# Causal maxima over blocks of 128 keys, a residual summed by a transfer, and the gate's logits copied before the next maximum

## The reference

```python
x = layernorm(x + local_attention(x))     # 16 heads of 8, each query sees itself and the 128 keys before it
x = layernorm(x + block(x))
# block: h = ln1(x); causal attention of h, 16 heads of 8, all earlier keys
#        x_resid = x + o @ w_o
#        moe_in = ln2(x_resid); probs = softmax(moe_in @ w_gate) over 8 experts; the best 2, renormalised
#        out = sum over the 2 of gate * (gelu(moe_in @ w1[e] + b1[e]) @ w2[e] + b2[e])
#        return out + x_resid
```

## Time and profile before

| | |
|---|---|
| median of 3 runs | 785.24 us (781.52 to 786.43) |
| the profiled execution | 784.6 us, its span 782.8 us, mean granted clock of TensorE 0.938 |
| PE busy | 632.5 us (81%) |
| DVE busy | 565.3 us (72%) |
| ACT busy | 461.5 us (59%) |
| POOL busy | 423.6 us (54%) |
| iterations 0 to 7 (local) | about 46 to 281 us |
| iterations 8 to 15 (causal) | about 281 to 586 us |
| experts and last norm | about 586 to 783 us |

### The profile page before, as it was taken

How to read it: one execution, slowest core, us unless ns; L and a number is a source line. 1 busy time by engine, 2 the same in 40 slices (tenths; PEclk the granted TensorE clock), 3 DMA queues, 4 the chain that set the end, 5 groups by cost and what they waited for, 6 DMA issues and landing times.

```text
span 782.8 us, 20450 instructions
## 1 busy us (share of the span) xinstructions
PE 632.5 (81%) x7679; PEld 386.4 (49%) x7679; DVE 565.3 (72%) x1302; ACT 461.5 (59%) x757; POOL 423.6 (54%) x646
## 2 busy tenths in 40 slices
PE   3568989988998788888888889888777996999760
PEld 1333444544454343444444434444337996899760
DVE  2655677877877989897879887989633784655573
ACT  2035666766765566766676767666773572555443
POOL 5026567666755544244646474657765556544672
PEclk8568999999999999999999999999998998999995
DMA  6745734754551626343526261710111223222745
GB/s 191 185 112 101 178 120 87 190 139 100 135 153 26 176 95 124 103 93 97 126 69 154 66 157 41 183 44 18 55 48 46 59 60 96 63 70 62 146 72 161
DMA packets 57549, 82.22 MB, mean 105 GB/s; under 512 B 7672, under 2 KB 48096, under 8 KB 54380
## 3 DMA queue, kind: packets, MB, share of 16 engines
q1 hardware_dynamic: 51228, 68.78, 35.0%
q0 software_dynamic: 5184, 11.61, 6.0%
q10 hardware_dynamic: 1040, 0.52, 0.2%
HBM read 43.55 MB, written 37.17 MB: 103 GB/s over the span
## 4 chain that ended last, share of the span: by engine, by line
PE 44%; DVE 17%; issue 11%; DMA 10%; ACT 8%; POOL 5%; SPq 3%; another core or an unknown queue 1%; POOLq 0%; DVEq 0%; ACTq 0%
PE side_ps L1473 9%; PE pair_ps L1622 8%; PE pair_ps L1634 7%; DMA arena<-parts_dram 5%; PE pair_ps L1393 4%; ACT probs L753 4%; PE pair_ps L1494 4%; DVE row_max L928 3%; POOL rows_dram L657 2%; DVE row_max L930 2%; DMA rows_dram<-rows,row_at 2%; DVE rest L951 2%; DMA arena<-shift_t 2%; PE pair_ps L1418 2%; PE pair_ps L1453 2%
## 5 line engine op out<-in xcount | busy, mean ns | idle before, releaser
L753 ACT ACTIVATE probs<-pair_ps 128x1024 f32<-128x1024 f32 x272 | 275.9, 1021 | 126.4 <-PE pair_ps L1393 123.2
L1473 PE MATMUL side_ps<-probs,v_aug 128*32 128x256 f32 (+3 forms) x2048 | 162.2, 412 | 9.1 <-POOL probs L645 4.0
L879 ACT ACTIVATE arena<-pair_ps,arena 128x128 f32<-128x128 f32 x284 | 81.0, 369 | 83.9 <-PE pair_ps L1622 60.4
L1393 PE MATMUL pair_ps<-arena 50*128 50x256 bf16 (+3 forms) x1024 | 107.6, 286 | 27.5 <-DMA arena<-shift_t 7.5
L632 POOL TENSOR_SCALAR_AFFINE_SELECT probs<-probs 128x512 f32<-128x512 f32 x96 | 61.4, 640 | 119.1 <-ACT probs L753 118.2
L698 POOL DMA_INDIRECT outputs_dram<-arena x71 | 71.0, 1000 | 73.4 <-DVE arena L1274 50.6
L919 DVE TENSOR_REDUCE row_max<-pair_ps 128x4 f32<-128x768 f32 x96 | 88.9, 950 | 26.4 <-PE pair_ps L1427 25.8
L1622 PE MATMUL pair_ps<-arena 128*128 128x128 f32 x568 | 80.3, 287 | 19.1 <-issue 10.1
L1393 PEld LDWEIGHTS pair_ps<-arena 50*128 50x128 bf16 x1024 | 32.4, 95 | 107.6 <-issue 43.7
L1622 PEld LDWEIGHTS pair_ps<-arena 128*128 128x128 f32 x568 | 73.0, 201 | 21.8 <-issue 21.7
L928 DVE TENSOR_REDUCE row_max<-pair_ps 128x2 f32<-128x1024 f32 x64 | 76.5, 1219 | 9.3 <-PE pair_ps L1453 7.7
(11 more groups left out here) (178 smaller groups left out, 1033.1 us busy)
## 6 DMA issues: line engine op xcount, KB each, us to landing
arena<-parts_dram SPq DMA_DIRECT2D x96, 192.0 KB
parts_dram<-parts SPq DMA_DIRECT2D x32, 384.0 KB
parts_dram<-parts SPq DMA_DIRECT2D x32, 256.0 KB
pack<-in_pack SPq DMA_DIRECT2D x8, 578.0 KB, 10.4
arena<-rows_dram SPq DMA_DIRECT2D x71, 65.0 KB
parts_dram<-parts SPq DMA_DIRECT2D x32, 128.0 KB
arena<-parts_dram SPq DMA_DIRECT2D x32, 128.0 KB
resid<-outputs_dram POOLq DMA_DIRECT2D x6, 512.0 KB
```

The source lines that it names most:

```text
L753: nc.scalar.activation(probs[:, n % PROBS, :], pair_ps[RING_AT["score", n][0]][:, :, :].rearrange("p b t -> p (b t)"), ACT.Exp, scale=SCAL ...
L879: last = nc.scalar.activation(hidden[n % H_DEPTH][:, f * BLK:(f + 1) * BLK], hidden_ps[n % 2][:, f * BLK:(f + 1) * BLK], ACT.Gelu_apprx_ta ...
L1393: last = nc.tensor.matmul(pair[:, r, col:col + width], k_st[u % STACKS][own, gs, j * P:(j + 1) * P], q_st[u % STACKS][own, gs, q0:q0 + wid ...
L1473: last = nc.tensor.matmul(o_ps[c * VHEAD:(c + 1) * VHEAD, q0:q0 + width], v_aug[u % 2][:, j, first:first + VHEAD], probs[:, slot, r * T + ...
```

## The change

Three edits, all in the causal units.

1. *Mixed pairs.* Each mixed pair is laid out as four blocks of 128 keys: queries 0 to 127 now stand in block 0 and the three blocks of queries 256 to 383 in blocks 1 to 3. One reduction writes a maximum per block, four per head slot, into a wider `row_max` (13 rows of results in place of 4). As queries 256 to 383 then have three partial maxima, `split_shift` first merges the three by one more reduction in SBUF, and waits for it. TensorE's mask product covers blocks 0 and 3 in place of 2 and 3, and the short product comes before the long one; their number and sizes stay.
2. *The residual.* GpSimd's addition of y into `resid` becomes an accumulating transfer on GpSimd's queue. `sum_ready` counts in sixteens.
3. *The logits.* The copy out of `misc` becomes a function of its own, `take_logits`. In step 16 VectorE runs it ahead of that step's maximum; the search for the two best stays behind it.

```diff
--- before.py
+++ after.py
@@ -272,7 +272,7 @@
         parts = sb("parts", [P, PARTS, 2, T], BF16)
         rest = sb("rest", [P, 2, T])
         v_aug = [sb(f"v_aug{i}", [P, NT, VROW]) for i in range(2)]
-        row_max = [sb(f"row_max{i}", [P, NT, TILES_R, GS]) for i in range(2)]
+        row_max = [sb(f"row_max{i}", [P, 3 * NT + 1, TILES_R, GS]) for i in range(2)]
         shift = sb("shift", [P, NT, TILES_R, 2, GS], BF16)
         shift_t = sb("shift_t", [4 * GS, T], BF16)
         probs = sb("probs", [P, PROBS, 2 * T])
@@ -382,7 +382,7 @@
         middle_ready, low_ready = sem("middle_ready"), sem("low_ready")
         stored_high, stored_low = sem("stored_high"), sem("stored_low")
         stack_in = [sem(f"stack_in{i}") for i in range(STACKS)]
-        max_filled, max_done = sem("max_filled"), sem("max_done")
+        max_filled, max_done, max_merged = sem("max_filled"), sem("max_done"), sem("max_merged")
         shift_hi, shift_lo = sem("shift_hi"), sem("shift_lo")
         shift_in = [sem(f"shift_in{i}") for i in range(STACKS)]
         score_filled, exp_done, masked = sem("score_filled"), sem("exp_done"), sem("masked")
@@ -670,7 +670,7 @@
 
                 b = w - B
                 pool.wait_ge(misc_taken, JOB["out", w])
-                nc.gpsimd.tensor_tensor(resid[:, b, :, :], y[:, :, :], resid[:, b, :, :], ALU.add).then_inc(sum_ready, 1)
+                nc.gpsimd.dma_start(resid[:, b, :, :], y[:, :, :], accum_op=ALU.add).then_inc(sum_ready, 16)
 
             for it in ITERATIONS:
                 w = it - 1
@@ -706,7 +706,7 @@
             def add_outputs(share, choice):
 
                 if (share, choice) == (0, 0):
-                    pool.wait_ge(sum_ready, B)
+                    pool.wait_ge(sum_ready, B * 16)
                     for i in range(X_DEPTH):
                         pool.wait_ge(y_out[i], len(range(i, SETTLED, X_DEPTH)) * 16)
                 if choice:
@@ -927,20 +927,25 @@
                 if m < 2:
                     nc.vector.tensor_reduce(top[:, 3, :, 2 * g + m], pair[:, :, :], AX_X, ALU.max).then_inc(max_done, 1)
                 elif m < 4:
-                    nc.vector.tensor_reduce(top[:, 2, :, 2 * g + m - 2], pair[:, :, 0:3 * P], AX_X, ALU.max)
-                    nc.vector.tensor_reduce(top[:, 0, :, 2 * g + m - 2], pair[:, :, 3 * P:T], AX_X, ALU.max).then_inc(max_done, 1)
+                    nc.vector.tensor_reduce(top[:, 0:3 * NT + 1:NT, :, 2 * g + m - 2], pair[:, :, :].rearrange("p b (n k) -> p n b k", k=P),
+                                            AX_X, ALU.max).then_inc(max_done, 1)
                 else:
                     nc.vector.tensor_reduce(top[:, 1, :, 2 * g:2 * g + 2], pair[:, :, :].rearrange("p b (s k) -> p b s k", k=2 * P),
                                             AX_X, ALU.max).then_inc(max_done, 1)
 
             def split_shift(u):
 
+                tops = row_max[u % 2][:, 0:NT, :, :]
                 dve.wait_ge(max_done, BEFORE[u + 1])
+                if layer(u) == CAUSAL:
+                    thirds = row_max[u % 2][:, NT:3 * NT + 1:NT, :, :]
+                    nc.vector.tensor_reduce(tops[:, 2, :, :], thirds.rearrange("p n r g -> p r g n"), AX_X, ALU.max).then_inc(max_merged, 1)
+                    dve.wait_ge(max_merged, u - B + 1)
                 if u:
                     dve.wait_ge(misc_filled, JOB["shift", u - 1])
-                nc.vector.tensor_scalar(shift[:, :, :, 0, :], row_max[u % 2][:, :, :, :], -1.0, None, ALU.mult).then_inc(shift_hi, 1)
+                nc.vector.tensor_scalar(shift[:, :, :, 0, :], tops, -1.0, None, ALU.mult).then_inc(shift_hi, 1)
                 dve.wait_ge(shift_hi, u + 1)
-                nc.vector.scalar_tensor_tensor(out=shift[:, :, :, 1, :], in0=row_max[u % 2][:, :, :, :], scalar=-1.0,
+                nc.vector.scalar_tensor_tensor(out=shift[:, :, :, 1, :], in0=tops, scalar=-1.0,
                                                in1=shift[:, :, :, 0, :], op0=ALU.mult, op1=ALU.subtract).then_inc(shift_lo, 1)
 
             def split_rest(u):
@@ -984,7 +989,7 @@
                     dve.wait_ge(x1_ready, B)
                     if b:
                         dve.wait_ge(applied, b)
-                        dve.wait_ge(sum_ready, b)
+                        dve.wait_ge(sum_ready, b * 16)
                     nc.vector.tensor_tensor(y[:, :, :], proj, resid[:, b, :, :], ALU.add).then_inc(misc_taken, 1)
 
             def moments(w):
@@ -1028,14 +1033,15 @@
                                                        ALU.subtract, ALU.mult)
                     last.then_inc(applied, 1)
 
-            def top_two(w):
-
-                b = w - B
-                done = b * len(ROUTE)
-                if b:
-                    dve.wait_ge(routed, done)
+            def take_logits(w):
+
+                if w > B:
+                    dve.wait_ge(routed, (w - B) * len(ROUTE))
                 dve.wait_ge(misc_filled, JOB["logits", w])
                 nc.vector.tensor_copy(logits[:, :, :].rearrange("p t e -> p (t e)"), misc[:, 0:NT * E]).then_inc(misc_taken, 1)
+
+            def top_two(w):
+
                 dve.wait_ge(misc_taken, JOB["logits", w])
                 for t in range(NT):
                     last = nc.vector.max(top_val[:, t, :], logits[:, t, :])
@@ -1229,6 +1235,8 @@
                         divide(w)
                     if "out" in before:
                         add_input(before["out"])
+                    if "logits" in before:
+                        take_logits(before["logits"])
                     for u, m in MAXIMA.get((it, k), ()):
                         maximum(u, m)
                     if project_at(it, k - 1) is not None:
@@ -1324,6 +1332,7 @@
                 if m == CHAIN["apply"]:
                     apply(LAST)
                 if m == CHAIN["logits"]:
+                    take_logits(LAST)
                     top_two(LAST)
                 if m == CHAIN["choose"]:
                     choose(LAST)
@@ -1431,18 +1440,15 @@
                     return
                 g, m = m // 5, m % 5
                 if m < 2:
-                    work, masked_cols = [(2 * g + m, 3, T, 0)], slice(3 * P, T)
+                    work, masked_blocks = [(2 * g + m, 3, T, 0)], slice(3, 4)
                 elif m < 4:
-                    work, masked_cols = [(2 * g + m - 2, 2, 3 * P, 0), (2 * g + m - 2, 0, P, 3 * P)], slice(2 * P, T)
+                    work, masked_blocks = [(2 * g + m - 2, 0, P, 0), (2 * g + m - 2, 2, 3 * P, P)], slice(0, 4, 3)
                 else:
-                    work, masked_cols = [(2 * g + s, 1, 2 * P, s * 2 * P) for s in range(2)], None
+                    work, masked_blocks = [(2 * g + s, 1, 2 * P, s * 2 * P) for s in range(2)], slice(1, 4, 2)
                 for half in range(2):
                     for r in range(TILES_R):
                         own = slice(HALF * r, HALF * (r + 1))
-                        if masked_cols is None:
-                            target = pair[:, r, :].rearrange("p (s k) -> p s k", k=2 * P)[:, :, P:2 * P]
-                        else:
-                            target = pair[:, r, masked_cols].rearrange("p (s k) -> p s k", k=P)
+                        target = pair[:, r, :].rearrange("p (s k) -> p s k", k=P)[:, masked_blocks, :]
                         keys = slice(HALF * half, P)
                         nc.tensor.matmul(target[:, :, keys], eye_b[own, HALF * (1 - half):HALF * (1 - half) + P],
                                          first_b[r][own, half, keys].unsqueeze(1).to_broadcast([HALF, target.shape[1], P - HALF * half]),
```

## The result

On the chip where the prediction was settled the changed kernel's median is 779.86 us against 785.13 us for the kernel before (18 runs each; 17 of the runs after lie from 776.96 to 781.80, and one execution of 1907.68 us stands outside and is not in the ratio): the ratio is 0.9932, 95% interval 0.9915 to 0.9948. Two more comparisons of the same two kernels gave 0.9941 (0.9914 to 0.9968) and 0.9929 (0.9902 to 0.9957). The forecast was 779.4 us. The gain is real, and under 1%. The profiled execution's span is 775.7 us, 7.1 us less than that of before.

The account below looks back on a forecast made before the run. The prediction took TensorE and VectorE, both nearly full in causal iterations and handing each other the maxima, as the bound. 784.6 - 3.4 - 1.5 - 0.9 = 778.8 us profiled, so a 779.4 us median; 8-in-10 range 772.5 to 786.5.

Parts of the forecast that it names:

- The logits: Step 16 of causal iterations: the copy moved past one maximum removes TensorE's 0.85 us stall in five iterations; 3.4 us gained.
- The clock: Behind step 16: with the stall gone, falls to 1.2 GHz become fewer; 1.5 us gained, bounds 2.5 gained and 2.5 lost.
- new falls would turn up elsewhere: Sign of being wrong: new falls of the clock in the local units or the experts, which the change doesn't touch.
- The mixed pairs: VectorE's mixed-pair reductions: 1.13 us from start to start, 0.06 less each, against small merges; 0.9 us gained.
- The residual: GpSimd's 1.28 us addition becomes a transfer's issue; 0 gained, bounds 1 us gained and 1 lost.
- the blocks cost more than two instructions: Rival, chance 0.1: each bank change costs VectorE, the reduction may take 1.6 us; total 792 us.
- the stall is only exchanged: Rival, chance 0.15: ScalarE, next to be late, holds TensorE and the clock falls as before; total 783.5 us.
- the clock doesn't hang on this stall: Rival, chance 0.1: the falls come from how the whole iteration is filled; total 780.9 us.
- More of it counts: Rival, chance 0.2: all clock falls go, the stall counts in full, plus VectorE's 2.3 us and 1 from the shift; 775.2 us.

Follow-up runs that it names:

- after_again: The changed kernel with all three edits, measured once more against the kernel before on the chip of other follow-up kernels: ratio 0.9941.
- after_third: The changed kernel with all three edits, measured again against the kernel before on a third chip: ratio 0.9929.
- logits_only: The kernel before with only the copy of the logits moved ahead of step 16's maximum: 758.03 us against 764.67, ratio 0.9923.
- mixed_only: The kernel before with only the mixed pairs in one reduction, plus the merge and TensorE's mask order: 762.75 us, ratio 0.9972.
- no_residual: The changed kernel with the residual's addition back on GpSimd: 779.37 us against the changed kernel's 782.3; ratio 0.9908 to the kernel before.
- rows_later_2: Repeat of the changed kernel with ScalarE's copy of the rows one step later: 777.26 us against the changed kernel's 782.3; 0.9865 of the kernel before.

## Why the prediction was right

The forecast was 779.4 us and 779.86 was measured. The mechanism was the forecast one, the stall for the logits and the clock behind it; that the number came out within 0.5 us is luck, since the terms measured one by one come to 8 us where 5.8 were forecast and 5.3 measured. By its own steps:

- **The logits** were put at 3.4 us, and the clock at 1.5. Alone the edit measured 5.9 (3.6 to 8.3), where the two steps are 4.9. The step was right in kind and low in size: the stall was worth 1.04 us and not 0.85, and 0.21 went back in each iteration and not 0.28 in three, which gives 5 x 0.83 = 4.1 us. How it goes back was read wrong. The prediction had ScalarE take 0.28 us in three iterations, and two in which the one-hot choice moves up by all of the stall and makes it good. At the exponential 0.34 us are taken back (2.32 us behind the turn, against 1.98), but the choice decides in all five: its end moves up by 0.81 of the 1.04 us, as GpSimd's masks, which follow ScalarE, stretch it from 0.44 to 0.69 us. In the two iterations of before in which TensorE shows a wait for it, that wait is 0.31 us now in place of 0.45, and the ranking still comes 0.21 us later behind the turn.
- **The clock.** The falls behind step 16 are gone in every trace. Three stood in the trace of before, 2.5 us by the prediction's count; the four kernels with the stall have 1.75 on average, at 1.0 us for a whole one, which is nearer to the 1.5 taken. By the rule cited from the Trainium skill (TensorE: Matmul & The Clock Gate, Part 1), taken alone, a half-busy array would have kept its clock; the runs show otherwise, with 7 falls behind 20 stalls with TensorE at work in 1.50 of the 3 us or just less, and none behind the 50 steps without one. The same Part 1 also describes a kernel in which brief idle times between groups of matmuls made the clock go back and forth, and with that the runs agree. That new falls would turn up elsewhere stood in the text as something that would make it wrong, and it half did, in the last causal iteration: 14 us at 1.2 GHz in all three traces of the changed kernel, 3.4 in the kernel before.
- **The mixed pairs** were put at 0.9 us and measured 2.1, with an interval (0.7 to 3.7) that takes in both; from the turn in iteration 8 to that in iteration 14 the trace is 3.4 us shorter, 2 of them falls. The reduction came out at 1.13 us from start to start, as taken, and the merge at 0.21 against 0.19. From the turn of the layer norm's output to the gate, where VectorE's chain of steps 12 to 15 seems to lie on the path (read from the order of the rows, not tested), it is 2.30 us in four of the five iterations after, against 2.49 to 2.73 before; but in after_again and after_third it is 2.30 in only two of five and 2.53 to 2.67 in the others. The iteration as a whole came to 38.3 to 38.5 us in the profiled execution, and 38.3 to 39.3 in the other two, where 39.5 was forecast.
- **The residual** at nothing was right, within what can be told: 1.0001 (0.998 to 1.0021) with the stall as cover, and without it no loss.
- Against these gains of some 8 us stand the 5.3 measured. No step of the forecast had this gap of 2 to 3 us. The intervals of the two edits alone nearly cover it, and falls of the clock are counted in both; the last causal iteration may have a share. Which of these it is stays open.

Of the rivals, "the blocks cost more than two instructions" is refuted by L930's 1219 ns, "the stall is only exchanged" by logits_only, and "the clock doesn't hang on this stall" by the 7 falls of 20 against none of 50. "More of it counts" was right that all falls go and that the stall counts in full, and wrong in the end, 775.2 us.

## What to carry to other kernels

Where several engines share a buffer in turns, look not for the long instruction but for the short one that frees the buffer and stands behind a long one: a copy of 0.18 us moved by one place was worth more than 56 instructions saved. A stall's price is not its idle time alone; look at the clock behind it, and at what stands second on the next engine, since moving ScalarE's copy of the rows by one step gained as much again (7.3 and 5.0 us). When an engine is moved, look also at what follows it: the masks on GpSimd followed ScalarE onto VectorE's one-hot choice, and took back 0.2 us of each 1.04. And to judge a change under 1%, measure a stretch between two fixed instructions: it separates an edit from the falls of the clock in code that nobody touched.

## What the runs showed of the hardware

- A reduction over PSUM that changes the bank with every run of 128 elements takes 1219 ns for 1024 elements, with 8 results scattered over `row_max` (L930 of the kernel after); with two runs and two results (L928) it takes the same 1219.
- VectorE's instruction from SBUF to SBUF that starts while GpSimd adds two float32 tensors in SBUF ends only about 0.05 us behind the addition: L941 and L946 (64 elements) take 0.53, 0.64, 0.78 and 1.21 us in place of 0.20, according to how much of the addition is left (before, mixed_only, no_residual). The one-hot instructions (32 elements) do the same behind a GpSimd mask that is already running, 0.33 and 0.43 us each, and take 0.19 when they start ahead of it (rows_later_2). Not every instruction is held: the merge L942, a reduction in SBUF, keeps its 0.21 us beside the addition, and reductions from PSUM their 1.21. The accumulating transfer's issue leaves L946 at 0.20.
- A matmul that had to wait shows less idle time than the wait costs: 0.85 us in its bracket, 1.04 us gained when the wait was gone (logits_only, after).
- The clock fell to 1.2 GHz behind 7 of 20 stalls, around which TensorE was at work in 1.47 to 1.50 of 3 us, and behind none of the 50 steps without the stall. A whole such fall costs an iteration 1.0 us.
- The kernel before takes 764 us in three of the five comparisons and 785 and 787 in the other two. From the last turn of the shift to the end, mostly the experts, it is 214 to 218 us in eight traces of the former and 234 to 238 in six of the latter.
